# Two hand-written step lists of a transformer block, put into another order

## The reference

```python
qkv = x @ Wqkv + bqkv                                  # 16 heads of 16
att = softmax(where(causal, q @ k.T / 4, -inf))
x = layernorm(x + (att @ v) @ Wout + bout)
h = silu(lin(x, w1) * s1) * (lin(x, w2) * s2)          # 256 -> 1024
h = gelu(lin(h, h1) * sh1)                             # 1024 -> 1024
h = gelu(lin(h, h2) * sh2)                             # 1024 -> 1024
out = layernorm(x + lin(h, w3) * s3)                   # 1024 -> 256
```

## Time and profile before

| | us |
|---|---|
| median of 3 runs | 2251.17 (2250.86 to 2251.55) |
| span of the profiled execution | 2245.9 |
| PE busy | 2155.0 (96%) |
| ACT, DVE, POOL busy | 1314.8, 1266.2, 490.6 |
| DMA | 167.72 MB, 74 GB/s from and to HBM |

### The profile page before, as it was taken

The page is one execution under the profiler, slowest core; times in us unless marked ns, Lnnn a source line. Parts: engine busy times, 40 slices in busy tenths (PEclk is TensorE's granted clock), DMA queues, the critical chain, the costliest instruction groups (busy, mean ns, idle before and its releaser), DMA issues.

```text
span 2245.9 us, 52053 instructions
## 1 busy us (share of the span) xinstructions
PE 2155.0 (96%) x16294; PEld 1874.6 (83%) x16294; DVE 1266.2 (56%) x3928; ACT 1314.8 (59%) x2807; POOL 490.6 (22%) x899
## 2 busy tenths in 40 slices
PE   7679999999999999999999999999999999999998
PEld 4348888888888889888888888889888888888898
DVE  6664655655555565555655565565555655555452
ACT  5446565665656666565665666566565665655553
POOL 2212222221221222122221222222122221221220
PEclk9869999999999999999999999999999999999999
DMA  7823232222322223232223323223232223322100
GB/s 254 277 66 73 56 72 66 71 68 69 83 62 68 71 69 77 65 77 71 61 70 79 74 54 74 65 65 77 65 78 68 62 69 80 77 51 52 32 6 10
DMA packets 95942, 167.72 MB, mean 75 GB/s; under 512 B 19204, under 2 KB 38404, under 8 KB 95672
## 3 DMA queue, kind: packets, MB, share of 16 engines
q1 hardware_dynamic: 88152, 141.22, 25.4%
q10 hardware_dynamic: 7520, 23.07, 2.9%
HBM read 98.26 MB, written 68.17 MB: 74 GB/s over the span
## 4 chain that ended last, share of the span: by engine, by line
PE 65%; issue 14%; DVE 3%; ACT 3%; DMA 3%; POOL 3%; SPq 2%; ACTq 0%; DVEq 0%; POOLq 0%
PE ring L1235 35%; PE ring L1220 7%; PE pO L1158 5%; PE pS L1098 4%; PE pM L1110 4%; PE ring L1170 4%; PE ring L1248 3%; DMA qk_d<-c 2%; POOL Xlo L689 2%; PE ring L1200 1%; ACT c L796 1%; DVE c L931 1%; ACT probs_b L765 1%; DVE full_g L954 1%; DVE x1Tlo L939 1%
## 5 line engine op out<-in xcount | busy, mean ns | idle before, releaser
L915 DVE CUSTOM_DVE_ANT_0 pM<-pM,mask 128x512 f32<-128x512 f32 (+3 forms) x1024 | 494.7, 505 | 350.2 <-PE pM L1110 281.2
L1235 PE MATMUL ring<-Yhi,H 128*128 128x256 f32 x1984 | 495.3, 286 | 6.1 <-DVE c L931 5.9
L1235 PE MATMUL ring<-Xhi,H 128*128 128x256 f32 x1984 | 497.6, 290 | 0.0
L1235 PE MATMUL ring<-Ylo,H 128*128 128x256 f32 x1984 | 487.9, 282 | 0.0
L1235 PE MATMUL ring<-Xlo,H 128*128 128x256 f32 x1984 | 483.8, 283 | 0.0
L1235 PEld LDWEIGHTS ring<-Yhi,H 128*128 128x128 f32 x1984 | 378.2, 191 | 16.0 <-issue 9.5
L1235 PEld LDWEIGHTS ring<-Xhi,H 128*128 128x128 f32 x1984 | 379.0, 191 | 4.5 <-issue 3.4
L1235 PEld LDWEIGHTS ring<-Ylo,H 128*128 128x128 f32 x1984 | 379.0, 191 | 3.3
L1235 PEld LDWEIGHTS ring<-Xlo,H 128*128 128x128 f32 x1984 | 379.8, 191 | 1.1
L1110 PE MATMUL pM<-Ks,Qs 128*128 128x512 f32 x992 | 287.2, 341 | 24.9 <-DVE mx L915 12.7
L859 ACT ACTIVATE Yhi<-ring,cols 128x256 fp32r<-128x256 f32 x248 | 117.4, 474 | 292.1 <-PE ring L1235 227.6
(11 more groups left out here) (148 smaller groups left out, 3554.5 us busy)
## 6 DMA issues: line engine op xcount, KB each, us to landing
qk_d<-c SPq DMA_DIRECT2D x120, 256.0 KB, 3.4
Qs<-qk_d SPq DMA_DIRECT2D x120, 192.0 KB
Ks<-qk_d SPq DMA_DIRECT2D x120, 192.0 KB
qk_d<-c SPq DMA_DIRECT2D x120, 128.0 KB, 3.1
xTs<-in_xT SPq DMA_DIRECT2D x16, 512.0 KB, 4.9
xz<-in_x SPq DMA_DIRECT2D x16, 512.0 KB, 4.0
raw<-in_h ACTq DMA_DIRECT2D x8, 1024.0 KB, 8.8
H<-raw ACTq DMA_DIRECT2D x8, 1024.0 KB, 13.6
```

The source lines that it names most:

```text
L915: nc.vector.tensor_tensor_reduce(pM[:, h % 2, 0:n], pM[:, h % 2, 0:n], mask[:, T - n:T], 1.0, NEG, ALU.add, ALU.max, mx[:, t, h:h + 1]).th ...
L1235: mm = nc.tensor.matmul(to, w, x_part, start=(k == 0 and m == 0), stop=(k == KB - 1 and m == 1))
```

## The change

It puts the steps of ORDER (326) and of HEAD_ORDER (250) into another order; FIRST_ORDER and TAIL_ORDER stay. Both lists hold the same steps before and after. The banks of `ring_banks` and the point at which the other engines' loop turns follow from the lists. The core of the diff, with the places that are spoken of below:

```diff
 ORDER = """
...
-exp:0:0:0 exp:0:0:1
...
-table:0:Exp:0 y:-1:0:0 y:-1:0:1 max:0:1:3:0 y:-1:1:0 h2:-2:1:0:0 exp:0:0:2 exp:0:0:3 y:-1:1:1 max:0:1:3:1
-exp:0:0:4 exp:0:0:5 h2:-2:1:0:1 exp:0:0:6 exp:0:0:7 max:0:1:3:2 exp:0:0:8 max:0:1:3:3 exp:0:0:9 h2:-2:1:1:0
...
-table:0:Exp:2 ln1:-1 ffn_out:-2:1:0 ffn_out:-2:1:1 exp:0:1:0 exp:0:1:1 qk:0:3 load_xT:1 max:0:2:3:0 exp:0:1:2
-max:0:2:3:1 exp:0:1:3 x1_turn:-1:0 exp:0:1:4 x1_turn:-1:1 exp:0:1:5 exp:0:1:6 max:0:2:3:2 max:0:2:3:3
...
-table:0:Exp:4 qk:1:0 exp:0:2:0 exp:0:2:1 h2:-1:0:0:0 h2:-1:0:0:1 exp:0:2:2 exp:0:2:3 max:0:3:3:0 h2:-1:0:1:0
-max:0:3:3:1 exp:0:2:4 exp:0:2:5 max:0:3:3:2 h2:-1:0:1:1 exp:0:2:6 max:0:3:3:3 exp:0:2:7 max:0:3:2:0 exp:0:2:8
-h2:-1:0:2:0 max:0:3:2:1 exp:0:2:9 max:0:3:2:2 exp:0:2:10 h2:-1:0:2:1 max:0:3:2:3 h_act:-1:h2:0:0
...
-table:0:Gelu:5 stack:1:0 h_act:-1:h2:0:1 h_rest:-1:h2:0:0 pv:0:2:1 o_out:0:2 h_act:-1:h2:0:2 max:0:3:1:0
...
-table:0:Exp:6 ffn_out:-1:0:0 ffn_out:-1:0:1 gu:-1:1:0 exp:0:3:0 exp:0:3:1 gu:-1:1:1 ffn_hi:-1:1:0 exp:0:3:2
-max:1:0:3:0 exp:0:3:3 max:1:0:3:1 gu:-1:1:2 exp:0:3:4 exp:0:3:5 ffn_hi:-1:1:1 gu:-1:1:3 ffn_hi:-1:1:2
...
-table:0:Gelu:7 pv:0:3:1 o_out:0:3 stack:1:1 max:1:0:2:0 h1:-1:1:0:0 max:1:0:2:1 h1:-1:1:0:1 h_act:-1:h1:1:0
...
-v:1:3 h_rest:-1:h1:1:2 h1:-1:1:3:0 h1:-1:1:3:1 h_act:-1:h1:1:3 max:1:0:0:0 rec_save:0 max:1:0:0:1
...
-h_act:-1:h1:1:6 den_turn:0 h_rest:-1:h1:1:6 ln2_stats:-1:0 h1:-1:1:7:0 h_act:-1:h1:1:7 h_rest:-1:h1:1:7
-h1:-1:1:7:1 ln2:-1:0 qk:1:2
+max:0:1:3:0 exp:0:0:0 y:-1:0:0 max:0:1:3:1 table:0:Exp:0 y:-1:0:1 y:-1:1:0 exp:0:0:1 exp:0:0:2 h2:-2:1:0:0
+exp:0:0:3 y:-1:1:1 exp:0:0:4 exp:0:0:5 h2:-2:1:0:1 exp:0:0:6 max:0:1:3:2 exp:0:0:7 max:0:1:3:3 exp:0:0:8
...
+h2:-2:1:6:1 h2:-2:1:7:0 h_rest:-2:h2:1:5 neg_split:0:1 ln1:-1 neg_max:0:1 h_act:-2:h2:1:7 h_rest:-2:h2:1:6
+h2:-2:1:7:1 h_rest:-2:h2:1:7 table:0:Exp:2 ffn_out:-2:1:0 x1_turn:-1:0 ffn_out:-2:1:1 exp:0:1:0 exp:0:1:1 qk:0:3
+exp:0:1:2 max:0:2:3:0 exp:0:1:3 max:0:2:3:1 exp:0:1:4 x1_turn:-1:1 exp:0:1:5 max:0:2:3:2 max:0:2:3:3 exp:0:1:6
+exp:0:1:7 gu:-1:0:0 gu:-1:0:1 exp:0:1:8 ffn_hi:-1:0:0 gu:-1:0:2 ffn_hi:-1:0:1 max:0:2:2:0 exp:0:1:9 stack:0:3
...
+max:0:3:3:0 h2:-1:0:0:0 ln2:-2:1 exp:0:2:0 max:0:3:3:1 exp:0:2:1 h2:-1:0:0:1 exp:0:2:2 exp:0:2:3 max:0:3:3:2
+h2:-1:0:1:0 exp:0:2:4 exp:0:2:5 h2:-1:0:1:1 max:0:3:3:3 exp:0:2:6 exp:0:2:7 h2:-1:0:2:0 max:0:3:2:0 exp:0:2:8
+max:0:3:2:1 exp:0:2:9 h2:-1:0:2:1 exp:0:2:10 table:0:Gelu:5 load_x:0 max:0:3:2:2 max:0:3:2:3 pv:0:2:1
...
+table:0:Exp:6 h_rest:-1:h2:0:7 qk:1:1 ffn_out:-1:0:0 ffn_out:-1:0:1 exp:0:3:0 exp:0:3:1 gu:-1:1:0 exp:0:3:2
+gu:-1:1:1 exp:0:3:3 ffn_hi:-1:1:0 gu:-1:1:2 max:1:0:3:0 exp:0:3:4 exp:0:3:5 gu:-1:1:3 ffn_hi:-1:1:1 exp:0:3:6
...
+gu:-1:1:6 exp:0:3:9 gu:-1:1:7 max:1:0:3:3 ffn_hi:-1:1:5 exp:0:3:10 ffn_hi:-1:1:6 v:1:0 max:1:0:2:0 pv:0:3:1
+stack:1:1 o_out:0:3 max:1:0:2:1 max:1:0:2:2 den:0 ffn_hi:-1:1:7 v:1:1 table:0:Gelu:7 h_act:-1:h1:1:0 h1:-1:1:0:0
...
+h_act:-1:h1:1:2 h_rest:-1:h1:1:1 h1:-1:1:1:1 h1:-1:1:2:0 h1:-1:1:2:1 v:1:2 max:1:0:1:3 h1:-1:1:3:0 rec_save:0
+h_act:-1:h1:1:3 max:1:0:0:0 h1:-1:1:3:1 max:1:0:0:1 h_rest:-1:h1:1:2 v:1:3 ln2_stats:-1:0 h_rest:-1:h1:1:3
+max:1:0:0:2 max:1:0:0:3 h1:-1:1:4:0 h_act:-1:h1:1:4 neg_split:1:0 h_rest:-1:h1:1:4 h_rest:-1:h1:1:5 h1:-1:1:4:1
+den_turn:0 rec_load:0 h1:-1:1:5:0 h1:-1:1:5:1 neg_max:1:0 h_act:-1:h1:1:5 h1:-1:1:6:0 h1:-1:1:6:1
+h_rest:-1:h1:1:6 h1:-1:1:7:0 h_act:-1:h1:1:6 h1:-1:1:7:1 h_rest:-1:h1:1:7 h_act:-1:h1:1:7 ln2:-1:0 qk:1:2
 """
 HEAD_ORDER = """
-raw:0:0 qk:0:0 qk:0:1 stack:0:0 max:0:0:3:0 table:0:Exp:0 max:0:0:3:1 stack:0:1 columns:0 raw:0:1 max:0:0:3:2
...
-exp:0:1:10 raw:0:9 max:0:2:0:3 neg_split:0:2 max:0:3:3:0 pv:0:1:1 o_out:0:1 qk:1:0 max:0:3:3:1 raw:0:10
-neg_max:0:2 max:0:3:3:2 max:0:3:3:3 exp:0:2:0 max:0:3:2:0 stack:1:0 exp:0:2:1 weights:0:6 max:0:3:2:1
...
-exp:0:2:10 max:0:3:0:3 neg_split:0:3 qk:1:1 weights:0:9 weights:0:10 weight_test:0:0 neg_max:0:3 max:1:0:3:0
-pv:0:2:1 o_out:0:2 stack:1:1 weight_test:0:1 weight_test:0:2 exp:0:3:0 exp:0:3:1 max:1:0:3:1 exp:0:3:2
...
-weight_test:0:10 v:1:2 low_bits:0 neg_max:1:0 rec_save:0 rec_load:0 exp:1:0:0 max:1:1:3:0 exp:1:0:1
...
+neg_split:0:0 max:0:1:3:0 raw:0:4 neg_max:0:0 max:0:1:3:1 qk:0:3 stack:0:3 raw:0:5 max:0:1:3:2 max:0:1:3:3
+weights:0:2 max:0:1:2:0 weights:0:3 v:0:1 max:0:1:2:1 v:0:2 v:0:3 max:0:1:2:2 max:0:1:2:3 max:0:1:1:0
+max:0:1:1:1 exp:0:0:0 exp:0:0:1 max:0:1:1:2 max:0:1:1:3 exp:0:0:2 exp:0:0:3 exp:0:0:4 max:0:1:0:0 exp:0:0:5
...
+table:0:Exp:0 neg_max:0:1 raw:0:6 load_xT:1 max:0:2:3:0 max:0:2:3:1 pv:0:0:1 max:0:2:3:2 max:0:2:3:3 exp:0:1:0
...
+max:0:2:1:1 weights:0:4 max:0:2:1:2 o_out:0:0 max:0:2:1:3 max:0:2:0:0 exp:0:1:6 qk:1:0 raw:0:7 max:0:2:0:1
+pv:0:1:0 exp:0:1:7 exp:0:1:8 exp:0:1:9 stack:1:0 max:0:2:0:2 max:0:2:0:3 exp:0:1:10 raw:0:8 weights:0:5
+neg_split:0:2 neg_max:0:2 qk:1:1 stack:1:1 o_out:0:1 raw:0:9 pv:0:1:1 max:0:3:3:0 max:0:3:3:1 exp:0:2:0
...
+max:0:3:1:3 max:0:3:0:0 pv:0:2:0 max:0:3:0:1 exp:0:2:9 weights:0:8 max:0:3:0:2 weight_test:0:0 exp:0:2:10
+max:0:3:0:3 weight_test:0:1 raw:0:10 neg_split:0:3 neg_max:0:3 weight_test:0:2 pv:0:2:1 max:1:0:3:0 exp:0:3:0
...
+neg_max:1:0 neg_split:1:0 rec_save:0 max:1:1:3:0 weight_test:0:8 max:1:1:3:1 max:1:1:3:2 exp:1:0:0 max:1:1:3:3
...
+max:1:1:0:0 max:1:1:0:1 max:1:1:0:2 max:1:1:0:3 neg_split:1:1 ln1:0 low_bits:0 o_out:1:0 neg_max:1:1 x1_turn:0:0
 """
```

More of the change, by code:

```diff
@@ new lines @@
+gu:-1:0:6 ffn_hi:-1:0:5 gu:-1:0:7 pv:0:1:1 h1:-1:0:0:0 ffn_hi:-1:0:6 max:0:2:2:3 max:0:2:1:0 ffn_hi:-1:0:7
+h1:-1:0:0:1 o_out:0:1 table:0:Gelu:3 h_act:-1:h1:0:0 h1:-1:0:1:0 h1:-1:0:1:1 h_rest:-1:h1:0:0 max:0:2:1:1
+h_rest:-1:h1:0:1 h1:-1:0:2:0 h_act:-1:h1:0:1 max:0:2:1:2 max:0:2:1:3 h_rest:-1:h1:0:2 h1:-1:0:2:1 h1:-1:0:3:0
+h1:-1:0:3:1 max:0:2:0:0 max:0:2:0:1 h1:-1:0:4:0 max:0:2:0:2 h1:-1:0:4:1 load_xT:1 h_act:-1:h1:0:2
+h_act:-1:h1:0:3 max:0:2:0:3 h1:-1:0:5:0 h_rest:-1:h1:0:3 neg_split:0:2 h_rest:-1:h1:0:4 h_act:-1:h1:0:4
@@ new lines @@
+h_rest:-1:h2:0:0 max:0:3:1:0 max:0:3:1:1 h_act:-1:h2:0:0 h_rest:-1:h2:0:1 h2:-1:0:3:0 h_act:-1:h2:0:1
+h_act:-1:h2:0:2 max:0:3:1:2 h2:-1:0:3:1 h2:-1:0:4:0 o_out:0:2 h_rest:-1:h2:0:2 max:0:3:1:3 h2:-1:0:4:1
+max:0:3:0:0 h_rest:-1:h2:0:3 h2:-1:0:5:0 max:0:3:0:1 stack:1:0 max:0:3:0:2 h2:-1:0:5:1 h_rest:-1:h2:0:4
+max:0:3:0:3 h_act:-1:h2:0:3 h2:-1:0:6:0 h_act:-1:h2:0:4 h2:-1:0:6:1 neg_split:0:3 h_act:-1:h2:0:5
+h_rest:-1:h2:0:5 h_act:-1:h2:0:6 neg_max:0:3 h2:-1:0:7:0 h_act:-1:h2:0:7 h_rest:-1:h2:0:6 h2:-1:0:7:1
@@ L141 @@
-max:1:1:1:0 o_out:1:0 max:1:1:1:1 y:0:0:1 y:0:1:0 y:0:1:1 ln1_stats:0 max:1:1:1:2 max:1:1:1:3 pv:1:0:1 ln1:0
-stack:1:2 max:1:1:0:0 max:1:1:0:1 max:1:1:0:2 max:1:1:0:3 neg_split:1:1 x1_turn:0:0 neg_max:1:1 x1_turn:0:1
+raw:0:0 qk:0:0 raw:0:1 load_x:0 qk:0:1 stack:0:0 max:0:0:3:0 max:0:0:3:1 weights:0:0 v:0:0 raw:0:2 max:0:0:3:2
+max:0:0:3:3 stack:0:1 columns:0 qk:0:2 max:0:0:2:0 max:0:0:2:1 max:0:0:2:2 max:0:0:2:3 raw:0:3 max:0:0:1:0
+stack:0:2 bias:0 max:0:0:1:1 weights:0:1 max:0:0:1:2 max:0:0:1:3 max:0:0:0:0 max:0:0:0:1 max:0:0:0:2 max:0:0:0:3
@@ new lines @@
+weight_test:0:5 pv:0:3:0 exp:0:3:10 pv:0:3:1 v:1:0 max:1:0:2:3 weight_test:0:6 max:1:0:1:0 max:1:0:1:1 o_out:0:3
+max:1:0:1:2 max:1:0:1:3 max:1:0:0:0 den:0 weights:0:10 max:1:0:0:1 weight_test:0:7 max:1:0:0:2 max:1:0:0:3
+neg_max:1:0 neg_split:1:0 rec_save:0 max:1:1:3:0 weight_test:0:8 max:1:1:3:1 max:1:1:3:2 exp:1:0:0 max:1:1:3:3
+weight_test:0:9 exp:1:0:1 exp:1:0:2 v:1:1 exp:1:0:3 exp:1:0:4 exp:1:0:5 max:1:1:2:0 rec_load:0 v:1:2 exp:1:0:6
+den_turn:0 max:1:1:2:1 max:1:1:2:2 exp:1:0:7 weight_test:0:10 exp:1:0:8 y:0:0:0 max:1:1:2:3 max:1:1:1:0 y:0:0:1
@@ L143 @@
+exp:1:0:9 exp:1:0:10 qk:1:2 y:0:1:0 max:1:1:1:1 v:1:3 max:1:1:1:2 y:0:1:1 max:1:1:1:3 ln1_stats:0 pv:1:0:1
+max:1:1:0:0 max:1:1:0:1 max:1:1:0:2 max:1:1:0:3 neg_split:1:1 ln1:0 low_bits:0 o_out:1:0 neg_max:1:1 x1_turn:0:0
+stack:1:2 x1_turn:0:1
 """
```

61 lines of the change are left out of this document (16 added, 45 removed).

## The result

The changed kernel takes **2233.18 us** (median of 4 runs, 2230.72 to 2237.98) against 2251.24 us (4 runs): ratio 0.9917, 95% interval 0.9902 to 0.9931. The forecast was 2226 us, with 2205 to 2248 as its range: faster, as forecast, but by 18 us, not 25. The two terms of the sum fared differently: the list of an iteration won a little more than forecast, and the list of the first batch's attention lost 7 to 9 us instead of winning 4.

A forecast was written before the change was run, and what follows sets the result against it. PE, 96% busy, was taken to bound the kernel, with 4.2 us of stalls an iteration to win from. -1.5 us times 14 iterations is -21, first batch -4: 2251.2 - 21 - 4 = 2226 us, range 2205 to 2248.

The forecast's parts named there:

- The end of an iteration: Iteration's seam: denominators sent 4.7 us sooner, ending the `den_turn` wait (-0.9 us) and the `rec_save` wait (-0.2 us).
- Exps against ACT: Iteration: PE's waits for ACT's exps thinned at three places, -0.9 of 2.9 us (0.25 + 0.25 + 0.4).
- What arises: Iteration's new stalls: less work over the save of `qk:0:3`, +0.3 us; later GELU table ahead of `h2:-1:0:3`, +0.2 us.
- The cap of 1.7 us: Iteration: PE's 98.7% matmul busy time would limit the gain to 1.3%, 1.7 us; weight-load share would not.
- First batch's attention: First 180 us: removed stack stall and moved tests against late exps and earlier tests, sum -4.4, taken as -4 us.
- late exps: First batch: group 0's exps behind `qk:0:3`, `stack:0:3` and three `v`, table load exposed: +5 us if nothing is hidden.
- tests +4.6: First batch: `weight_test` 0 and 1, 2 x 2.3 us on DVE, ahead of `neg_split:0:3`, for which PE waits.
- stall for the stack: First batch: PE's 9.97 us wait for `stack:1:0` near 80 us goes entirely, -10 us.
- late tests: First batch: last three tests and `low_bits`, 4 x 2.3 us, move behind `neg_split:1:0` into DVE's gaps: -4 us.
- The round trips decide: Rival, chance 0.12: transfers with less work over them cost +1.0 us an iteration, +8 at the start: 2273 us.
- The stalls only move: Rival, chance 0.10: PE waits for the same results one step later, 0 an iteration: 2247 to 2251 us.
- More of the stock goes: Rival, chance 0.12: exp places and seam empty nearly all, -2.1 to -2.9 us an iteration, -12 at first: 2198 us.

The follow-up runs named there:

- e5: Kernel before with only the end of an iteration's list, behind `max:1:0:3:3`, in the new order: 2256.15 us, ratio 1.0033.
- e9: Kernel before with the second gate half and the end of an iteration's list in the new order: 2224.84 us, ratio 0.989.
- e7: Kernel before with only the middle 112 steps of an iteration's list, `ffn_out:-2:1:0` to `exp:0:2:9`, in the new order: 2268.65 us, ratio 1.0093.
- e12: As e11, with `qk:0:3` in the iteration's list moved two steps up, ahead of `exp:0:1:0`: 2222.18 us, ratio 0.9877 to the kernel before.
- e2: Changed kernel with the old list of an iteration, keeping the first batch's new list: 2257.92 us, ratio 1.0034 to the kernel before.
- e4: Changed kernel with the first batch's `qk:1:1` back behind `neg_split:0:3` and `stack:1:1` behind `o_out:0:2`: 2225.83 us.
- e8: Changed kernel with e3's and e4's edits, and the first batch's `weight_test` 0 and 1 put back behind `neg_max:0:3`: 2218.08 us.
- e3: Changed kernel with the first 78 steps of the first batch's list in the old order: 2222.39 us, ratio 0.987 to the kernel before.
- e11: As e8, with the first batch's `weight_test` 7 also moved, from ahead of `max:1:0:0:2` to behind `neg_split:1:0`: 2220.02 us.

## Why the prediction was right, and where it was wrong

**The end of an iteration** (-0.9 and -0.2 us): right. e5 and e9 have -0.90 at the start, e9 and the whole list -0.30 at the end; a further -0.24 at the start comes with group 0's order. The rows that answer, SP and DVE of after:

```profile
1038.70 3.32 SPq L604 DMA_DIRECT2D Oc<-Osb  x4
1042.07 0.54 SPq L605 DMA_DIRECT2D den_d<-Osb  x1
1043.80 0.35 SPq L610 DMA_DIRECT2D dn<-den_d  x1
...
1048.93 1.35 SPq L618 DMA_DIRECT2D rec<-rec_d  x2
```

```profile
1046.87 0.55 DVE L954 RECIPROCAL dn<-dn 128x64 f32<-128x64 f32 x1
...
1055.41 1.29 DVE L958 TENSOR_TENSOR Oc<-Oc,rec 128x512 f32<-128x512 f32 x2
```

`den` goes out behind `o_out:0:3` with no `stack` between, 5.1 us after its first transfer instead of 6.75 (1.65 us sooner, where 3.4 were taken for the `stack`). `rec` comes 6.5 us before `den_turn`, and neither the reciprocal nor `den_turn` has idle time ahead of it (0.45 and 2.57 us before). What the step left out is the rest of that segment: that `max:1:0:2:0` moves up too, and that only the new gate half keeps it from costing 1.15 us net (e5). The term held for the pair of segments and not for the segment alone; as the prediction doesn't speak of these maxima, that was luck.

**Exps against ACT** (-0.9): right in sum. Group 0 brings -0.24 and costs 0.11 behind it, group 2 -0.17 with the bank below in it, the second gate half -0.5 to -0.8 where -0.4 was taken. The weight loads' waits for ACT are 15.6 us in ten iterations, lower than the 20 forecast. For `x1_turn` nothing was taken; it is -0.19 in the whole list and +0.80 in e7, without the earlier `ln1`.

**What arises** (+0.3 and +0.2): right. The first gate half has +0.19 to +0.47 in the profiles that hold the new list, all of it behind `exp:0:1:9`, and e12 takes it off by moving `qk:0:3`. DVE's first write of `full_g` waits for the save in two iterations that follow one another:

```profile
967.75 0.48 DVE L942 SCALAR_TENSOR_TENSOR full_g<-ring,cols,th 128x256 f32<-128x256 f32 x1 [0.67 <-DMA qk_d<-c]
...
1100.86 0.48 DVE L942 SCALAR_TENSOR_TENSOR full_g<-ring,cols,th 128x256 f32<-128x256 f32 x1 [2.27 <-DMA qk_d<-c]
```

0.38 us in the earlier trace rows; in every second iteration it is now 0.9 to 2.3 us, in those between 0.7, so "2 or so" is right for a few. The bank behind the GELU table costs 0.13 us a mean iteration at `h2:-1:0:3` (before: none).

In sum -1.5 was forecast; the period fell by 1.3 us by the reciprocals, by 2.0 in iterations 4 to 13 and by 23.6 / 14 = 1.7 us by "rest". The Trainium skill ("Perfetto Trace Analysis", section Identifying the Most-Contended Engine) calls PE's busy share a poor measure of headroom, and this trace agrees. Iterations 4 to 13 in before and after (columns as in the earlier trace rows):

```profile
523.80:1866.00 1342.20, 1321.58 (x10162) 1161.06 (x10161) 766.61 (x2441) 809.94 (x1740) 297.95 (x550) 1.00 0.28 70
530.20:1852.20 1322.00, 1311.85 (x10163) 1161.04 (x10161) 762.21 (x2441) 817.06 (x1740) 300.92 (x550) 1.00 0.29 71
```

They became 20.2 us shorter, but PE's idle time fell by 10.5 us only (20.6 to 10.2): half of the gain lay in time that the matmuls' records count as busy. The cap of 1.7 us in the prediction was taken from 500 to 1000 us; in these ten iterations the idle time of before is 2.1 us each, and the gain of 2.0 stays just under it.

**First batch's attention** (-4, bounds -12 and +8): wrong in sign, and in these two profiles 1 us beyond the bound (+6.9 by the medians of e2). The forecast named its own sign of failure, `weight_flag` after 152; it came at 157.7. By PE's starts, before and after:

| stretch | before | after | difference | forecast |
|---|---|---|---|---|
| to `neg_max:0:1` | 49.27 | 58.93 | +9.7 | late exps, +5 |
| to `neg_max:0:2` | 14.71 | 15.12 | +0.4 | |
| to `neg_max:0:3` | 15.84 | 27.14 | +11.3 | tests +4.6; `qk:1:1` nothing |
| to `exp:0:3:0` | 14.27 | 4.10 | -10.2 | stall for the stack, -10 |
| to `weight_flag` | 54.52 | 52.43 | -2.1 | late tests, -4 |
| sum | | | +9.1 | -4.4 |

The stack's 10 us and the tests' 4.6 (5.32 read as a wait, 4.5 between e4 and e8) were right. For the late tests the sum took four moves; only `weight_test` 8 and 9 pass `neg_split:1:0`, as test 10 and `low_bits` stood behind it before too. And the 1.4 us more that the prediction names for a drain besides the table load are not in the trace of before: from an exp's end to the GELU behind the load it is 1.31 us (1003.81 to 1005.12), of which the load is 1.28.

Two steps failed. The late exps were sized by what moves ahead of them (+5, "if none of it is hidden"); the stretch costs 9.7. The 4.4 us of it that are PE's idle time are near that price; the other 5.2 us are matmuls at a lower clock, for which the sum has no term, though the earlier trace rows show 0.97 for that stretch in before. And the prediction let the moves on SP pass as "nothing" without asking what `qk:1:1` needs: it followed `stack:1:0` on SP and not `qk:1:1` on ACT, where the one tile `c` still waits for the landing of the save before. e3 and e4 show that price, 5.7 to 6.2 us. e8 adds that the -10 for the stack was itself partly bought by PE being late: with PE early again 3.5 us of the stall return (4.9 in e11).

**Rivals.** "The round trips decide" was meant for the iteration, where it did not decide, and is part of what happened in the first batch: at `qk:1:1` a landing, not an engine, ended the waits. "The stalls only move" is true of e7 and of e12, and not of the whole. "More of the stock goes" had -2.1 to -2.9 us an iteration; the -1.7 to -2.0 read lie between it and the forecast.

The total is the sum of both: an iteration's list 2.6 us better than its -21, a first stage 13.1 us worse than its -4, and 3.5 us by which the profiled execution of before was faster than its median; 2226 - 2.6 + 13.1 - 3.5 = 2233 us. The sign rests on the iteration's list; with the first stage's error alone it would have been 2239 us, still in the range.

## What to carry to other kernels

In a hand-ordered list price a segment, not a step: what a step gains can hang on another step that empties the bank or writes the operand earlier, and undoing or doing one of them alone says little (two of three parts of this list slow the kernel by themselves, one pair holds all of the gain). For every moved step that saves a tile to DRAM ask when that tile is free again, and follow the in-order engine that stands there first. In a stage that runs once, do it with the landing times and the granted clock of that stage, not with those of the steady loop: where PE has gaps, compare its busy time for the same matmuls too, not only the waits.

## What the runs showed of the hardware

The same four matmuls (128x512) took 1.88 us at a granted clock of 1.00 and 3.48 us at 0.50. Of the 9.7 us that the first batch loses up to `neg_max:0:1`, about half is this and not waits; e3, with the old 78 steps, has PE idle for 13.4 instead of 17.5 us there and the clock at 1.00 throughout. What brings the clock down there wasn't settled.

A save's landing takes different times. While the weights were loaded, ACT waited until 82.27 us for copies of which the last had been sent from 73.31 to 75.14, so 7.1 us; in an iteration the save of `qk:0:3` had landed 2.7 us after its last copy was sent (964.47 + 0.61 to 967.75). What else is on the queues is the obvious difference, but no run separates it. It also differs between neighbouring iterations with the same order: 4.3 us in the next one (1095.98 + 0.60 to 1100.86). The last copies on SP in after:

```profile
964.47 0.61 SPq L519 DMA_DIRECT2D qk_d<-c  x1
...
1095.98 0.60 SPq L519 DMA_DIRECT2D qk_d<-c  x1
```

The stall of PE that follows stands in every second iteration alone, in after as in e11; why the landing alternates wasn't settled.
